# A decoder block with cross-attention on one core: the units between the scores of a batch are put in a new order

## The reference

```python
x = layernorm(x + linear_attention(x))             # 16 heads of 8, 32 features
x = layernorm(x + cross_attention(x, ctx, ctx))    # below
x = layernorm(x + ffn(x))                          # 512 wide, with a sine
# cross-attention of one batch, 16 heads of 8:
q, k, v = q @ Wq.T + bq, k @ Wk.T + bk, v @ Wv.T + bv
scores = einsum('bhqd,bhkd->bhqk', qh, kh) / sqrt(8)
out = einsum('bhqk,bhkd->bhqd', softmax(scores), vh)
y = concat(out) @ Wo.T + bo
```

## Time and profile before

| | |
|---|---|
| median of 3 runs | 783.1 us (775.49 to 784.4) |
| profiled execution | 776.4 us, span 774.5 us |
| TensorE clock granted, mean | 0.952 of full |
| PE busy | 696.1 us, 90% of the span |
| DVE busy | 585.0 us, 76% |
| ACT busy | 571.9 us, 74% |
| POOL busy | 455.3 us, 59% |

### The profile page before, as it was taken

The page is one execution under the profiler, slowest core; times in us unless marked ns, Lnnn a source line. Parts: engine busy times, 40 slices in busy tenths (PEclk is TensorE's granted clock), DMA queues, the critical chain, the costliest instruction groups (busy, mean ns, idle before and its releaser), DMA issues.

```text
span 774.5 us, 33301 instructions
## 1 busy us (share of the span) xinstructions
PE 696.1 (90%) x12468; PEld 450.6 (58%) x12468; DVE 585.0 (76%) x1147; ACT 571.9 (74%) x1143; POOL 455.3 (59%) x491
## 2 busy tenths in 40 slices
PE   6878867398999999999999999999999999997884
PEld 3555542165656666666666666666666666665553
DVE  4677757376778887888888888878878888884498
ACT  3547742287788888888888888888888888887772
POOL 6401152467667667777777766677677777620462
PEclk9889986599999999999999999999999999997997
DMA  7001127627678787877777778786777777750001
GB/s 210 1 2 41 41 62 160 141 82 141 144 140 154 147 151 147 154 139 154 154 174 153 149 150 148 148 157 141 142 154 165 171 142 152 138 108 3 3 0 48
DMA packets 39404, 93.18 MB, mean 120 GB/s; under 512 B 7880, under 2 KB 14536, under 8 KB 39368
## 3 DMA queue, kind: packets, MB, share of 16 engines
q1 hardware_dynamic: 39368, 92.69, 59.0%
HBM read 66.06 MB, written 26.54 MB: 120 GB/s over the span
## 4 chain that ended last, share of the span: by engine, by line
PE 72%; DVE 10%; ACT 8%; issue 6%; DMA 1%; POOL 1%; SPq 1%; ACTq 0%; DVEq 0%; POOLq 0%
PE psum L952 15%; PE psum L979 13%; PE psum L996 11%; PE psum L940 9%; PE psum L1002 8%; PE psum L932 6%; ACT probs L697 4%; PE psum L852 2%; DVE mx L1250 1%; PE psum L838 1%; PE psum L960 1%; DVE k_stack L1391 1%; ACT k L717 1%; DVE rden L1185 1%; DVE stats_f L1315 1%
## 5 line engine op out<-in xcount | busy, mean ns | idle before, releaser
L1250 DVE TENSOR_REDUCE mx<-psum 128x1 f32<-128x500 f32 x672 | 421.4, 672 | 118.2 <-PE psum L952 115.3
L697 ACT ACTIVATE probs<-psum 125x448 f32<-125x448 f32 x768 | 376.0, 543 | 88.0 <-PE psum L979 87.4
L952 PE MATMUL psum<-kh,q_max 64*128 64x500 f16 (+1 forms) x672 | 177.1, 386 | 3.9 <-DVE mx L1250 3.6
L979 PE MATMUL psum<-q_diag,k_stack 64*128 64x112 f16 x3072 | 155.8, 213 | 12.9 <-ACT probs L697 5.6
L996 PE MATMUL psum<-probs,v_ext 125*32 125x112 f32 x3072 | 150.2, 268 | 0.0
L979 PEld LDWEIGHTS psum<-q_diag,k_stack 64*128 64x128 f16 x3072 | 99.2, 95 | 81.3 <-ACT probs L697 49.2
L1002 PE MATMUL psum<-probs,v_ext 125*32 125x112 f32 x3072 | 145.4, 262 | 0.0
L537 POOL CAST kh<-k 128x500 f16<-128x500 f32 x96 | 57.7, 601 | 120.4 <-ACT k L717 120.3
L525 POOL TENSOR_TENSOR c_hl<-c_in,c_hl 128x500 f16<-128x500 f32 x96 | 109.9, 1145 | 7.7
L543 POOL TENSOR_TENSOR kl<-k,kh 128x500 f16<-128x500 f32 x96 | 106.4, 1136 | 0.2
L996 PEld LDWEIGHTS psum<-probs,v_ext 125*32 125x32 f32 x3072 | 74.5, 110 | 31.5 <-issue 21.7
(11 more groups left out here) (147 smaller groups left out, 693.2 us busy)
## 6 DMA issues: line engine op xcount, KB each, us to landing
k_stack<-k_halves SPq DMA_DIRECT2D x192, 187.5 KB, 6.3
c_in<-ctx_in SPq DMA_DIRECT2D x32, 750.0 KB, 5.4
k_halves<-kh SPq DMA_DIRECT2D x32, 375.0 KB, 5.8
k_halves<-kl SPq DMA_DIRECT2D x32, 375.0 KB, 6.3
q_stack<-q_halves SPq DMA_DIRECT2D x32, 64.0 KB, 2.3
q_diag<-mT SPq DMA_DIRECT2D x64, 0.8 KB
q_diag<-mT SPq DMA_DIRECT2D x64, 0.1 KB
out<-x_all SPq DMA_DIRECT2D x8, 112.0 KB
```

What stands on the lines that cost most here:

```text
L697: nc.scalar.activation(probs[0:KP, t % PBUF, half * 2 * GC:(half + 1) * 2 * GC], scores[k % RING_AT][0:KP, 0:2 * GC], ACT.Exp, scale=SCALE ...
L952: last = nc.tensor.matmul(bank[:, 0:CH], q_max[u][rows, r * P:(r + 1) * P], kh[u][rows, c * CH:(c + 1) * CH], start=True, stop=True)
L979: mm = nc.tensor.matmul(scores[(2 * t + half) % RING_AT][:, g * PAIR:(g + 1) * PAIR], k_stack[u][rows, g, t * KP:t * KP + P], q_diag[u][ro ...
L1250: dve.tensor_reduce(mx[:, r * KC + c:r * KC + c + 1], bank[:, 0:CH], AX.X, ALU.max).then_inc(mx_done, 1)
```

## The change

Three tables get new values. `PLAN`: part two of every step is empty. Part one holds M units alone, up to four, and part three, behind the two value products, holds all K2, V, X, T, Z and Y units and the M units that are left. `M_ORDER` now has an M on rows 0 to 63 and one on rows 64 to 127 side by side, with r = 3 between such pairs. `PAIRS` has nine entries for six.

```diff
-M_ORDER = ((3, 0), (0, 0), (1, 0), (4, 0), (5, 0), (2, 0), (6, 0), (0, 1), (1, 1), (4, 1), (5, 1), (2, 1),
-           (6, 1), (3, 1), (0, 2), (4, 2), (3, 2), (1, 2), (5, 2), (2, 2), (6, 2))
-PAIRS = (8, 14, 17, 19, 2, 5)
+M_ORDER = ((0, 0), (4, 0), (1, 0), (5, 0), (3, 0), (2, 0), (6, 0), (0, 1), (4, 1), (1, 1), (5, 1), (3, 1),
+           (2, 1), (6, 1), (0, 2), (4, 2), (1, 2), (5, 2), (2, 2), (6, 2), (3, 2))
+PAIRS = (0, 2, 5, 7, 9, 12, 14, 16, 18)
 SHARED = MB // 2
-PLAN = ((("M1", "M1", "M1", "K2"), ("M1",), ("M1",)),
-        (("M1", "M1", "V"), ("M1", "M1"), ("T",)),
-        (("M1", "K2", "M1", "M1"), (), ("M1", "M1")),
-        (("K2", "Z"), (), ("X",)),
-        (("M2", "V", "M2"), ("M2", "M2"), ("Y",)),
-        (("M2", "V", "M2", "M2"), (), ()))
+PLAN = ((("M1", "M1", "M1", "M1"), (), ("K2", "M1")),
+        (("M1", "M1", "M1", "M1"), (), ("V",)),
+        (("M1", "M1", "M1", "M1"), (), ("M1", "K2")),
+        ((), (), ("K2", "T", "X")),
+        (("M2", "M2", "M2", "M2"), (), ("M2", "V", "Z")),
+        (("M2", "M2"), (), ("V", "Y")))
```

## The result

The changed kernel takes 844.65 us (842.32 to 845.56, 4 runs) against 781.25 us for the kernel before, run beside it (775.49 to 784.4, 4 runs). The ratio is 1.0816 [1.0744, 1.0888]. The forecast was 845 us with a range of 820 to 872. The profiled execution took 844.19 us, with a span of 842.3 us.

What follows compares the result with a forecast made beforehand. PE was taken to bound the kernel before; after the change, waits through ACT's copies would, 20.01 us a body against 17.86. 30 x 2.15 = 64.5 us and about 1 more on 776.4 gave 842, adjusted to 845 us, range 820 to 872.

Steps and rivals of the forecast that it cites:

- the tie that was forecast: Step 1's second pair gets its bank 4.0 us after score(0), its score due at about 4.3; costed at nothing.
- The step that failed: Each step: the next exponential waits behind ACT's copy, the second score behind that exponential; 3.22 us with V, 3.18 with K2.
- the first rival: PE stays the bound and fewer, denser M products make the kernel faster: 702 to 744 us; chance 4%.
- This wait goes: The first K2's wait for POOL's split after the last V, 8.0 us in all, disappears; V to K2 becomes 3.22 us.
- The rival of 13%: Bursts of M also wait for banks, DVE 0.3 us late at steps 1 and 5: 0.6 us a body more, 863 us.
- the ring: Waits from second score through value products, V or K2, ACT's copy and exponential to the next second score: +2.15 us a body.
- the rival of 6%: PE's small idle gaps in the loop lower the clock; a tenth of 180 steps gives +36 us, 881 us; chance 6%.

Runs made afterwards that it cites:

- e10: Changed kernel with the loop's V and K2 copies cut to a quarter of their columns: 828.62 us, ratio 1.0597 to the kernel before.
- e4: Changed kernel with each V copy of the loop on ACT cut to a quarter of its columns: 836.14 us, ratio 1.0741 to the kernel before.
- e7: Changed kernel with bursts of two M for four, the other M behind K2 or V in part three: 886.63 us.
- e9: Changed kernel with the K2 of step 3 put back between that step's scores: 827.95 us, ratio 1.0594 to the kernel before.
- e1: Changed kernel, nine pairs kept, with the copies and their units back between the two scores of a step: 793.11 us.
- e8: Kernel before with eight M pairs for six, V first in step 4 and another M order: 786.25 us, ratio 1.008.
- e12: Kernel before with seven M pairs for six through the order of M alone, PLAN unchanged: 787.45 us, ratio 1.0106.
- e2: Kernel before with its three V units moved behind the value products, K2 left in place: 848.77 us, ratio 1.0914.
- e6: Changed kernel with, on ACT alone, the first half of exp(2m+2) put ahead of part three's copies: 903.71 us, ratio 1.1623.

## Why the prediction was right

**The steps.** From second score to second score, medians of bodies 8 to 27. T, Z and Y come in every other body:

| step | forecast | with T, Z, Y | without |
|---|---|---|---|
| 0 | 3.18 | 3.31 | 3.24 |
| 1 | 3.22 | 3.18 | 3.18 |
| 2 | 3.40 | 3.51 | 3.43 |
| 3 | 3.67 or 3.42 | 3.62 | 3.36 |
| 4 | 3.44 | 3.39 | 3.39 |
| 5 | 3.22 | 3.35 | 3.21 |

The sum was 20.01, the body is 20.08. Part of that closeness is luck, since small errors cancel. The value products take 0.91 us ahead of V, K2 and M alike, for 0.85, and K2 to its copy 0.93 for 0.85 (393.35 to 394.28). V's copy to the exponential takes 0.48 for 0.59. Y isn't hidden and costs 0.13. In step 0 the bank wait of 0.33 us (395.21) ends as the exponential lets the score go anyway: the tie that was forecast.

**What bounds a step.** The place of the waits and the length of the steps were as forecast, but the copy was given too large a part. The step that failed reads "score(2m+2) can go ... but exp(2m+2) stands behind the copy". The exponential stands behind the score as well, and the score behind the copied unit: 0.30 + 0.91 + 0.77 + 0.48 + 0.60 = 3.06 us for 3.18, and 3.06 is what this step takes in e10. Both paths end within 0.12 us in this V step, so the forecast's number held with either. The forecast came out right with the wrong one of two paths in front. e4, e7 and e10 tell them apart, and the starts of the scores (PE L979) show it for the whole loop, in us a body, means of bodies 8 to 27:

| kernel | from first to second score, six times | from second score to the next first | sum |
|---|---|---|---|
| before | 8.49 | 9.19 | 17.68 |
| changed | 7.08 | 12.99 | 20.07 |
| e10, short copies | 6.59 | 12.98 | 19.57 |
| e9, one K2 back | 7.00 | 12.36 | 19.36 |
| e7, M moved out | 6.65 | 14.60 | 21.25 |

The shortest way from a first score to its second is 1.07 or 1.08 us in each of the fourteen kernels; six of them are 6.5. So of the work moved out from between the scores, 3.8 us a body came on top outside and only 1.4 fell away inside. Short copies act on the first column alone, and can't take it below 6.5; putting a unit back acts on the second. The cause as shown is this: between the two scores PE has at most 0.65 us of work, and the score, exponential, score chain takes 1.08 or more (1.20 with a V copy in front, at 397.43, and 1.35 with a K2 copy in front, at 400.78). The work that used to fill that time now stands where ACT has nothing left to do. The same error would have made a wrong forecast for e7, and did.

A caution on reading such rows: step 5, from 388.93 to 392.14, runs over the turn of the loop. There the exponential comes 0.62 us behind its score, and in e10, with the short copy, it is 0.62 too (383.71 to 384.33). ACT's branch and register instructions of the turn lie in between (the last at 391.45), and the views don't list them. That 0.12 us is not the copy's.

**The nine pairs.** -1.1 us a body if PE were the bound: not seen anywhere. e1 (body +0.49), e8 (+0.47) and e12 (+0.12) have more pairs with the units between the scores, and none is shorter than before. So the gain that I had given to the pairs and to the first rival was too high: it had a lone M at the full price of a pair. Its other part, 0.11 us for each change of depth, was a wrong reading. In both kernels two value products take 0.90 to 0.91 us to whatever follows, a score, an M of either depth, K2, V or T; only X follows after 0.79. So the 0.11 belongs to X and not to the depth. A change shows elsewhere: from an M on all 128 rows to a score it is 0.31 us (393.99 to 394.30), from a pair on half the rows 0.24 (395.21 to 395.45).

**POOL.** "This wait goes": 8.0 us to 2.2, right, and e2 shows what it would have been with K2 left in its place, 39.1.

**Banks.** The rival of 13% is there, and bursts that wait for L1250 were a sign of being wrong: 18.9 us in all, one of them at 395.21. But the steps came out as forecast without it, so the ring hides most of it. In e6 bank waits aren't hidden, those for ACT's copies above all, and the loss is 59 us.

**Clock.** 1.00 in every window from 200 to 760 us, so the rival of 6% did not come. The Trainium skill, "TensorE: Matmul & The Clock Gate", section "A second HAM failure mode: psum-queue depth-cycling", tells of a kernel in which small idle times took the clock down and up. The trace doesn't show that here: PE was idle for 11.8 us in 100, in pieces of up to 1.0, at the full 2.4 GHz.

**Two signs that missed.** PE's waits for exponentials were to pass 100 us and came to 77.3; there were 142 of them for some 168 second scores, 0.54 us in the mean, as forecast. The busy share was to be near 80%, and 88.20 us in 100 were measured. The durations in the rows overlap, and a product of 0.37 us that ends before a wait fills part of what the starts show as waiting.

## What to carry to other kernels

When two engines pass a buffer back and forth, first read how long the round takes (here score, exponential, score: 1.1 us), and keep that much independent work of the first engine inside it; work moved out of the round adds its length outside, while inside a wait takes its place. When two chains end close together, name both before costing an edit: a forecast by either gives the same time, and the wrong one points to the wrong remedy (shorter copies, 0.5 us a body; one unit put back, 0.7). A unit that another engine's long chain starts from (the last V) has to be moved together with the unit at that chain's end (the first K2).

## What the runs showed of the hardware

The granted clock fell at the loop's end rather than in its gaps. Four windows of e9 in its last bodies (columns as above; the clock is the third number from the end):

```profile
730.00:740.00 10.00, 9.00 (x210) 5.90 (x202) 7.56 (x15) 7.57 (x16) 0.89 (x1) 1.00 0.85 149
740.00:750.00 10.00, 5.40 (x80) 3.50 (x82) 5.36 (x32) 3.55 (x9) 0.00 (x0) 0.73 0.22 26
750.00:760.00 10.00, 7.91 (x115) 6.23 (x107) 0.58 (x2) 5.49 (x11) 0.00 (x0) 0.59 0.01 2
760.00:770.00 10.00, 6.83 (x102) 5.10 (x103) 4.75 (x14) 6.01 (x11) 1.27 (x1) 0.58 0.01 2
```

PE was busy for 9.00 of the first 10 us at clock 1.00, then for 5.40 with 0.73 granted. Bodies 30 and 31 have less work beside the scores. Means of 0.59 and 0.58 say that the clock was mostly at its lower level of 1.2 GHz there, and the distance of their output copies went from 20.2 us (e8) to 29.8 (e9). So up to 9.6 us of a total has nothing to do with the body, and kernels whose bodies differ by under 0.3 us are compared by the body. That is so for e12, with 0.12 us a body and 25.4 us for that distance against 20.3 before.

ACT's read of PSUM shortens with the columns, but not in proportion: 0.58 us for 125 x 512 and 0.27 for 125 x 128.
